# Window attention on one core: keys and values as differences to key 0, scores with features on partitions

## The reference, cut to what matters

```python
def window_attn(x, Wqkv, bqkv, scale, ws=2, nh=8):          # 128 channels, 8 heads of 16
    xw = windows of 2 x 2 pixels                             # 4 tokens a window
    qkv = (xw @ Wqkv + bqkv)                                 # q, k, v per head
    attn = softmax(q @ k.T * scale)                          # 4 queries x 4 keys per head
    return attn @ v
...
x -> group norm (32 groups of 4 channels, no weights)        # input (4, 128, 32, 32)
xr = xn.reshape(B, H, W, C)                                  # a plain reshape of the memory
g = window_attn(xr) @ Wproj + bproj
l = 2 x 2 mean of xn, again window_attn on 16 x 16 pixels
l = blur in y + blur in x, resized bilinearly to 32 x 32
return x + (g + l).transpose(0, 3, 1, 2)
```

## Time and profile before

| | us |
|---|---|
| runs, lowest / median / highest | 103.12 / 103.97 / 104.14 |
| span of the profiled execution, first to last instruction | 101.1 |
| PE busy | 87.2 |
| DVE busy | 82.4 |
| POOL busy | 51.4 |
| ACT busy | 45.6 |

### The profile page before, as it was taken

The page is one execution under the profiler, slowest core; times in us unless marked ns, Lnnn a source line. Parts: engine busy times, 40 slices in busy tenths (PEclk is TensorE's granted clock), DMA queues, the critical chain, the costliest instruction groups (busy, mean ns, idle before and its releaser), DMA issues.

```text
span 101.1 us, 1874 instructions
## 1 busy us (share of the span) xinstructions
PE 87.2 (86%) x647; PEld 79.8 (79%) x647; DVE 82.4 (81%) x137; ACT 45.6 (45%) x99; POOL 51.4 (51%) x43
## 2 busy tenths in 40 slices
PE   4949899989947998799999998589999994999960
PEld 1927589979947996799999996479999983999920
DVE  0062906999989999997979999999999999989770
ACT  3160247935862744864578505851613451222110
POOL 6201004499696930099999369729189549000000
PEclk9999999999998599999999999999999999999998
DMA  1699500000000000000000000005000004000072
GB/s 54 181 406 394 209 0 0 0 6 0 0 0 3 0 3 0 6 0 0 0 0 6 0 0 0 0 0 207 6 0 0 0 0 172 36 6 3 0 306 109
DMA packets 2313, 5.35 MB, mean 53 GB/s; under 512 B 513, under 2 KB 897, under 8 KB 2305
## 3 DMA queue, kind: packets, MB, share of 16 engines
q1 hardware_dynamic: 2016, 4.92, 12.7%
q10 hardware_dynamic: 288, 0.33, 1.1%
HBM read 3.15 MB, written 2.10 MB: 52 GB/s over the span
## 4 chain that ended last, share of the span: by engine, by line
PE 45%; DVE 21%; issue 13%; POOL 9%; DMA 5%; ACT 3%; SPq 0%; DVEq 0%; ACTq 0%; POOLq 0%
PE sm_ps L858 7%; PE ot_ps L882 6%; DVE sm_ps L674 6%; PE k_ps L823 6%; DMA x_sb<-in_x 5%; DVE qk L640 5%; POOL pv L387 5%; PE v_ps L847 5%; PE q_ps L823 3%; PE job_ps L802 2%; POOL qk L387 2%; PE ot_ps L776 2%; DVE out_sb L705 2%; PE v_ps L788 2%; PE ot_ps L788 2%
## 5 line engine op out<-in xcount | busy, mean ns | idle before, releaser
L387 POOL TENSOR_TENSOR pv<-pv 128x1024 f32<-128x1024 f32 (+1 forms) x11 | 21.6, 1964 | 8.3 <-DVE pv L691 7.9
L691 DVE TENSOR_TENSOR pv<-sm_ps,v_sb 128x2048 f32<-128x2048 f32 x9 | 20.6, 2290 | 0.3
L640 DVE TENSOR_TENSOR qk<-q_ps,k_sb 128x512 f32<-128x512 f32 x32 | 20.8, 679 | 0.0
L462 POOL TENSOR_TENSOR qk<-q_sb,k_sb 128x512 f32<-128x512 f32 x8 | 10.3, 1289 | 11.3 <-ACT q_sb L551 8.0
L387 POOL TENSOR_TENSOR qk<-qk 128x1024 f32<-128x1024 f32 (+1 forms) x7 | 15.5, 2217 | 0.2
L858 PE MATMUL sm_ps<-ident,qk 128*128 128x128 f32 x108 | 13.6, 274 | 1.3 <-POOL qk L387 1.2
L858 PEld LDWEIGHTS sm_ps<-ident,qk 128*128 128x128 f32 x108 | 11.9, 141 | 1.8 <-issue 1.7
L882 PE MATMUL ot_ps<-ident,pv 128*128 128x128 f32 x80 | 10.5, 274 | 2.5 <-POOL pv L387 1.9
L882 PEld LDWEIGHTS ot_ps<-ident,pv 128*128 128x128 f32 x80 | 9.0, 141 | 3.7 <-issue 3.3
L674 DVE TENSOR_TENSOR sm_ps<-expd,inv 128x128 f32<-128x128 f32 x10 | 10.1, 1011 | 0.3
L580 ACT ACTIVATE ot<-ot_ps,bias_v 128x512 f32<-128x512 f32 x10 | 6.9, 687 | 7.6 <-PE ot_ps L882 7.6
(11 more groups left out here) (88 smaller groups left out, 146.5 us busy)
## 6 DMA issues: line engine op xcount, KB each, us to landing
x_sb<-in_x SPq DMA_DIRECT2D x3, 512.0 KB, 7.1
out<-out_sb SPq DMA_DIRECT2D x3, 512.0 KB, 2.6
resize_sb<-in_resize SPq DMA_DIRECT2D x1, 640.0 KB, 7.3
x_sb<-in_x SPq DMA_DIRECT2D x2, 256.0 KB, 4.9
out<-out_sb SPq DMA_DIRECT2D x2, 256.0 KB, 2.0
w_sb<-in_L_conv_Wqkv ACTq DMA_DIRECT2D x1, 192.0 KB, 5.6
bias_rows<-in_L_conv_bqkv ACTq DMA_DIRECT2D x1, 128.0 KB, 4.6
wp_sb<-in_L_conv_Wproj SPq DMA_DIRECT2D x1, 64.0 KB, 6.6
```

The lines of the kernel that those rows point to most:

```text
L387: return engine.tensor_tensor(low, low, high, ALU.add)
L462: nc.gpsimd.tensor_tensor(*query_key_operands(n, i, q_sb[:, n % 2, :], i - WIN + POOL_QUERIES), ALU.mult).then_inc(qk_pool, 1)
L640: ins = nc.vector.tensor_tensor(*query_key_operands(n, i, q_ps[n % 2][:, :], i), ALU.mult)
L691: nc.vector.tensor_tensor(to, a, b, ALU.mult).then_inc(pv_dve, 1)
```

## The change

**Layout.** Features lie on partitions for `Q` and `K`. Of the four tokens of a window, the normalising step leaves token 0 as it is and the other three as differences to it, so that keys 1 to 3 and values 1 to 3 come out as differences to key 0 and value 0. The score against key 0 is a constant zero, written once into columns 0 to 63 of the bank (`zero`). Three keys instead of four are multiplied: 1536 products a tile, in one instruction (L523), and 1536 of probabilities by values (L568). Value 0 is added in `O` by a transpose of its own.

**Scores.** The sum over a head's features is a matmul with a 0/1 matrix of 32 columns: 4 queries by 4 groups of 32 windows, 192 columns each, for two tiles at once (L706). The softmax runs once for two tiles, on 256 columns; its result is brought back to windows on partitions by two DVE transposes of 32 x 32 blocks (L554).

**Key sums.** POOL does two additions of 512 elements for each tile (`H`, `H2`; L275), tile 8 has the first alone, tile 9's is on DVE. The halvings of scores are gone.

**Input.** Rows are images by pairs: batches 2p and 2p + 1 of half of the channels lie in xr[:, 2p], the other half in xr[:, 2p + 1]. The first tile needs both, and its four tokens turned. For images 2 and 3, ACT scales (`part`, `base`) and POOL subtracts (L379). POOL pools the images (L353, L357). x is loaded a second time, as channels, for the residual. The bias of keys is gone (only differences count), and the query's is added by ACT.

**Output.** All eight `out` jobs are the same, each half an image through the one bank `job_ps`.

```diff
 ORDER = {
...
-        ("bn", 0), ("mean", 0), ("var", 0), ("norm", 0, 1), ("norm", 0, 0), ("bn", 1), ("mean", 1), ("var", 1),
+        ("bn", 0), ("mean", 0), ("bn", 1), ("var", 0), ("mean", 1), ("norm", 0, 1), ("var", 1), ("norm", 0, 2),
...
             def keys(n):
-                pe.wait_ge(k_seeded, n + 1)
-                product(n, 1, k_ps).then_inc(k_made, 1)
+                inputs_turned(n)
+                if n >= 2:
+                    pe.wait_ge(qk_done, n - 1)
+                to = k_ps[n % 2][:, 0:KEYS * NW]
+                nc.tensor.matmul(to, w_sb[:, C:2 * C], all_tokens(n, 1), start=True, stop=True).then_inc(k_made, 1)
             def queries(n):
-                pe.wait_ge(q_seeded, n + 1)
-                product(n, 0, q_ps[n % 2]).then_inc(q_made, 1)
+                inputs_turned(n)
+                if n >= 1:
+                    pe.wait_ge(q_out, n)
+                nc.tensor.matmul(q_ps[:, :], w_sb[:, 0:C], all_tokens(n, 0), start=True, stop=True).then_inc(q_made, 1)
-            def sum_scores(n):
-                products_done(pe, n)
-                terms = HD >> sums_halved(pe, ("HS", "HS2"), n)
...
+            def sum_scores(m):
+                pe.wait_ge(qk_done, 2 * m + 2)
...
+                for q in range(WIN):
+                    for g in range(4):
+                        rows = slice(32 * g, 32 * (g + 1))
+                        ins = nc.tensor.matmul(s_ps[rows, 64:256], head_sum[:, q, :], qk[:, m % 2, q, :, :, rows],
+                                               start=(q == 0), stop=(q == WIN - 1), skip_group_check=True)
             def sum_values(n):
...
+                for q in range(WIN):
+                    to = view[:, q // 2, q % 2]
+                    nc.tensor.matmul(to, v0_sb[:, n % V0BUF, :], eye, is_transpose=True, start=True, stop=False,
+                                     skip_group_check=True)
+                    for k in terms:
+                        ins = nc.tensor.matmul(to, pv[:, n % 2, q, k, :], eye, is_transpose=True, start=False,
+                                               stop=(k == terms[-1]), skip_group_check=True)
+            def query_key(n):
+                m = n // 2
+                dve.wait_ge(q_out, n + 1)
+                dve.wait_ge(k_made, n + 1)
+                if m >= 2:
+                    dve.wait_ge(s_made, m - 1)
...
+                nc.vector.tensor_tensor(qk[:, m % 2, :, :, n % 2, :], q, k, ALU.mult).then_inc(qk_done, 1)
+            def divide(m):
...
+                for half in range(2):
+                    nc.vector.transpose(
+                        prob_w[:, m % 2, half, :].rearrange("w (q k h) -> w k q h", q=WIN, k=KEYS),
+                        prob[:, m % 2, :].rearrange("r (k t w) -> r t k w", k=KEYS, t=2)[:, half]).then_inc(turn_done, 1)
             def prob_value(n):
+                dve.wait_ge(turn_done, n + 1)
+                dve.wait_ge(v_made, n + 1)
+                dve.wait_ge(v0_out, n + 1)
+                if n >= 2:
+                    dve.wait_ge(ot_made, n - 1)
...
+        def sums_of_keys(eng, engine, kind, n):
...
+            first, other = pv[:, n % 2, :, 0, :], pv[:, n % 2, :, 1 if kind == "H" else 2, :]
+            return engine.tensor_tensor(first, first, other, ALU.add)
+            def normalise(p, j):
+                pool.wait_ge(part_done, 1 + j)
+                at = 0 if j == 1 else 1
+                nc.gpsimd.tensor_tensor(xn[:, p, j, :], part[:, j, :], base[:, at, :],
+                                        ALU.subtract).then_inc(normed[p][j], 1)
         def bank(job):
-            if job == ("out", LAST - 1, 1):
-                return k_ps
-            if job[0] in ("low", "begin", "end"):
-                return v_ps if job[2] else q_ps[0]
+            if job[0] in ("mean", "var"):
+                return v_ps[1]
+            if job in (("xt", 0, 0), ("xt", 0, 2)):
+                return ot_ps
             return job_ps
```

More of the change, by code:

```diff
@@ L43 @@
 F32 = mybir.dt.float32
-BF16 = mybir.dt.bfloat16
 B, C, H, W = 4, 128, 32, 32
@@ L275, in conv_attention_kernel @@
+        summed = {(e, k): sem(f"summed_{e}_{k}") for e in ("POOL", "DVE") for k in ("H", "H2")}
         job_made, job_act, job_dve = sem("job_made"), sem("job_act"), sem("job_dve")
@@ new lines, in jobs_read, with key_sums @@
+        def jobs_read(eng, item, its_bank):
+            jobs = [j for j in among(ORDER["PE"][:ORDER["PE"].index(item)], ("mean", "var", "xt", "lt", "out"))
+                    if bank(j) is its_bank]
+            if jobs:
+                job_read(eng, jobs[-1])
+        def key_sums(eng, kinds, n):
+            times = 0
+            for kind in kinds:
+                for e in ("POOL", "DVE"):
+                    if (kind, n) in ORDER[e]:
+                        eng.wait_ge(summed[e, kind], sum(j[0] == kind and j[1] <= n for j in ORDER[e]))
+                        times += 1
+            return times
@@ L544, in queries_out @@
             def queries_out(n):
                 act.wait_ge(q_made, n + 1)
-                if n >= 2:
-                    products_done(act, n - 2)
-                first = min([job[2] for job in ORDER["POOL"] if job[:2] == ("M", n)] + [WIN - 1])
-                nc.scalar.copy(q_sb[:, n % 2, (first - WIN + POOL_QUERIES) * C:],
-                               q_ps[n % 2][:, first * C:]).then_inc(q_out, 1)
+                act.wait_ge(bias_loaded, 48)
+                if n >= QBUF:
+                    act.wait_ge(qk_done, n - QBUF + 1)
@@ L688, in prob_value @@
[L688 to L700 removed]
+                shape = [P, WIN, KEYS * HEADS, HD]
@@ new lines, in prob_value, with result @@
+                p = prob_w[:, n // 2 % 2, n % 2, :].rearrange("w (q kh) -> w q kh", q=WIN)
+                v = v_ps[n % 2][:, C:].rearrange("w (kh d) -> w kh d", d=HD)
+                nc.vector.tensor_tensor(pv[:, n % 2, :, :, :].rearrange("w q k (h d) -> w q (k h) d", d=HD),
+                                        p.unsqueeze(3).broadcast_to(shape), v.unsqueeze(1).broadcast_to(shape),
+                                        ALU.mult).then_inc(pv_done, 1)
+            def result(b, half):
+                job = ("out", b, half)
@@ L722, in _ @@
             PE = ORDER["PE"]
-            OUT_FIRST = among(PE, ("out", "low"))[0]
-            def jobs_read(item, its_bank):
-                jobs = [j for j in among(PE[:PE.index(item)], ("xt", "lt")) if bank(j) is its_bank]
-                if jobs:
-                    job_read(pe, jobs[-1])
-            def job_begins(job):
-                earlier = [j for j in JOBS[:JOBS.index(job)] if bank(j) is bank(job) and j[0] != "low"]
-                if earlier:
-                    job_read(pe, earlier[-1])
+            OUT_FIRST = among(PE, ("out",))[0]
@@ L737, in do_job @@
+            K_FIRST = among(PE, ("K",))[0]
+            def job_begins(job):
+                its_bank = bank(job)
+                jobs_read(pe, job, its_bank)
+                at = PE.index(job)
+                if its_bank is ot_ps:
+                    done = len(among(PE[:at], ("O",)))
+                    if done:
+                        pe.wait_ge(ot_out, done)
             def do_job(job):
                 job_begins(job)
-                values_before, values_summed = before(PE, job, ("V",)), before(PE, job, ("O",))
@@ L772, in do_job @@
[L772 to L789 removed]
+                    _, p, j = job
@@ L790, in do_job @@
                 else:
                     _, b, half = job
-                    low = POOLED[b // 2]
-                    tiles = [TILES.index((b, t)) for t in range(HALVES)]
-                    if kind in ("out", "low"):
-                        blocks = [i for i, (k, _) in enumerate(BLOCKS) if k // (K // 2) == half]
-                        pe.wait_ge(ot_out, low + 1)
-                        for i in blocks:
-                            k, l = BLOCKS[i]
-                            at = (k - half * K // 2) * C
-                            low_ot = ot[:, low, :].rearrange("f (b l c) -> f b l c", b=2, l=KL)[:, b % 2, l]
-                            ins = nc.tensor.matmul(bank(job)[:, at:at + C], resize_sb[:, i, :], low_ot,
-                                                   start=(i == blocks[0]), stop=True, skip_group_check=True)
@@ L804, in do_job @@
-                    for t in {"low": (), "out": (0, 1), "begin": (0,), "end": (1,)}[kind]:
-                        pe.wait_ge(ot_out, tiles[t] + 1)
-                        ins = nc.tensor.matmul(
-                            bank(job)[:, :].rearrange("f (k t c) -> f t k c", t=HALVES, c=CH)[:, t], wp_sb[:, :],
-                            ot[:, tiles[t], :].rearrange("f (h k c) -> f h k c", h=2, c=CH)[:, half],
-                            start=False, stop=True, skip_group_check=True)
+                    low, tile = TILES.index((None, b // 2)), TILES.index((b, half))
@@ new lines, in do_job @@
+                    if job == OUT_FIRST:
+                        pe.wait_ge(wp_loaded, 16)
```

(9 more changed lines are left out.)

764 lines of the change are left out of this document (345 added, 419 removed), and 49 rows, old and new, of the table ORDER.

## The result

The changed kernel takes 123.06 us (median of 4 runs, 121.96 to 124.52), against 104.06 before: 1.183 times as long, 95% interval 1.173 to 1.193. The forecast was 121.3, slower, within 107 to 134. The profiled execution is the slowest of the four, 124.52 with a span of 122.8; the other three had spans of 120.2 to 121.9.

What follows compares the result with a forecast made beforehand. VectorE was taken as the bound of the kernel before, TensorE close behind. For the change, 84.75 us up to the end stretch plus 33.6 gave 118.35; with 2.9 added, 121.3 us, range 107 to 134.

Steps and rivals of the forecast that it cites:

- Prices: Instruction times from the profile's rows; VectorE's work per pair of tiles 9.65 us, before some 13.
- `S`: Score sums on TensorE, 32 instructions of 192 columns: 2.2 us, with 1.3 and 5.3 as ends.
- The start: Before the first product: both input rows needed and pooling hindering VectorE, so first product at 24.0 instead of 16.6.
- The first pair: From first product at 24.0: first division waits for the third variance behind K2 and Q2, until 33.1.
- The middle: GpSimd's key sums behind waiting subtractions, then TensorE at half clock: VectorE idle 15.6 us.
- The end: After VectorE's last product: output jobs through one bank and late order, 33.6 us to the end.
- Around the span: Distance from the profiled span to the runs' median, 2.9 us, added to the sum.
- C: Whole kernel: VectorE stays the bound, 105.7 us, or 100.2 with shorter scores and earlier first product; chance 0.13.
- B: Score sums: column groups run one after another, 5.3 us each, +3.1 at five places, 137 us; chance 0.13.
- D: End: TensorE falls to half clock at output jobs, 135 us, or 128 for half of them; chance 0.10.

Runs made afterwards that it cites:

- the repeated kernel: The changed kernel run once more without any edit, as yardstick for later kernels on the same chip: 123.09 us.
- the kernel with the middle orders: Changed kernel with GpSimd's key sums earlier, third scores earlier on TensorE and third exponent earlier on ScalarE: 108.99 us, ratio 1.052.
- the last kernel: Changed kernel with middle orders, four output banks, later pooling, reordered end, and earlier second and third variance: 97.31 us, ratio 0.933.
- the first experiment: Changed kernel with only GpSimd's order edited, key sums of tiles 0 and 1 ahead of subtractions: 111.63 us, ratio 1.075.

## Why the prediction was right, step by step

- **Prices.** VectorE's products were within 2% (1.73 and 1.75 for 1536), its busy time is 66.6 where 68 was forecast, and the two block transposes took 0.44 together where I had 0.56. In the softmax the sum took 0.60 instead of 0.50 and the reciprocal 0.55 instead of 0.5; with the transposes the division came out at 2.0 as forecast.
- **`S`** was taken at 2.2 from the spacing of tiny matmuls, and took 1.51. By the Trainium skill, page TensorEngine Tiling (Array Packing), section Key Properties, different tiles work in parallel, which gave 1.3; the trace is nearer to that, and so are the loads shown above. This is the term with the largest relative miss: up to 0.7 too much at four of the places, but the third sum took 2.79 at half clock, 0.6 more than I had. On the path that is at most 2 us, an estimate from these differences.
- **The start** was 2.4 too early in the profiled execution (26.37 instead of 24.0) and 1.7 in the repeated one. In the first the second half of the first rows came at 7.32 instead of 6.68; in the other it came at 6.54, so that the 1.7 has other causes: GpSimd hindered VectorE fully, not half (1.0), and the rest lies in the turned inputs and first products. The Trainium skill, page SBUF — State Buffer, section Who interferes with whom, says that `tensor_scalar` can contend too; the trace agrees, 1.25 us beside the pooling against 0.48 for the other `base` without it.
- **The first pair.** I let K2 and Q2 run at full clock, and had 9.1 us from the first product to the first division. In the profiled execution they ran at half clock (1.65 and 1.73 us) after pauses of 1.24 and 1.18 us; VectorE waited 2.33 for `var 2`, and it became 10.0. In the repeated kernel they ran at full clock (0.91 and 1.02), and it was 8.3. So this 1.65 us differs from one execution to the next, and no run here shows what decides it.
- **The middle** was right in place, cause and size: idle 2.73, 12.26 and 1.71 where 2.95, 11.25 and 1.35 stood, GpSimd's first key sum at 51.17 behind L379, 7.1 us late where I had 7.4. Undone by one line, 11.2 us went; with TensorE's and ScalarE's orders, 13.5.
- **The end** was right: 33.4 us from VectorE's last product (86.01, two of them, to 89.39) to the end of the span, where 33.6 stood. Of its two causes the single bank is worth 5.5. For the other I wrote that before the change three output jobs were done ahead of the last scores; by the order table of the kernel before they are four, and with the change two.
- **Around the span** I added 2.9, the distance from the profiled span to the median of other runs. Here the runs lie 1.7 to 1.8 above their own spans. Against my span of 118.35 the measured ones are 2.05 above in the repeated kernel and 1.9 to 4.5 above in the four runs; the 1.2 too much around the span cancels a part of this. That 121.3 is as near to 123.06 as it is, is in so far luck.
- **Rivals.** C (VectorE stays the bound) was not what happened. The nearest to it with the one bank is the kernel with the middle orders, 108.99 where C said 105.7. In the last kernel VectorE is busy for 41.1 of the 45 us from 30 to 75, close to C's picture, but its 97.31 has four banks as well, and is no test of C's 100.2. B was settled by the 1.51. D (half clock in the end) did not come in the changed kernel: from 70 to 110 us the clock is 1.00, and 0.93 in what is left. My argument against it was wrong, though: TensorE's pauses there are not under 1 us but up to 2.52, the clock stayed at 1.00 after that one, and in the first experiment it fell after one of 2.51.

Of the 19 us lost, the middle is 13.5 and the single bank 5.5. With the start (about 3) these are more than the whole loss, so that something else in the change is a gain that they covered. That it is VectorE's lighter work fits its 15.8 us less, but no run separates it from the rest of the change.

## What to carry to other kernels

When an order by hand is rewritten, follow every engine's queue for what a shared one now has in front of its first link: here GpSimd's key sums behind two subtractions cost 11.2 us, against 15.8 us of work that VectorE was spared. The largest wait of a profile names its last releaser, not its cause; moving the scores forward removed a wait of 12.3 us and no time. And the pauses can be paid twice, once as pauses and once in TensorE's clock, as they were in the middle here.

## What the runs showed of the hardware that was not expected

- The same 16 f32 matmuls with 32-column weights (32 instructions of 192 columns) took 1.51 us with neighbours in different columns and 3.53 with neighbours in the same ones, at full clock. Inside one group of columns the spacing was 0.16 us in both; the next group started 0.68 us after the one before, ahead of that one's last loads.
- The third scores took 2.79 at a granted clock of 0.50, 1.85 times as long, with pauses of 5.5 and 4.2 us ahead on TensorE. With these filled by matmuls the clock stayed at 1.00.
- One kernel's clock differs between executions: behind pauses of 1.24 and 1.18 us it was 0.74 from 30 to 35 us in the profiled execution, and behind 0.82 and 1.18 it was 1.00 there in the repeated kernel.
- GpSimd's additions of 512 elements took 1.04 in the pooling, 1.48 for the one that ran beside VectorE's two tokens, and 1.28 in the key sums.
